# Seven half products in place of eight for queries, keys and gate of a linear attention, one pair of heads ahead

## The chip, the cores and the metric

The kernel runs on one core of a Trainium2 chip, as one launch. The metric is the device time of the whole program in microseconds (us). An engine name is short for: PE = TensorE matmul, PEld = its weight load, DVE = VectorE, ACT = ScalarE, POOL = GpSimd, SP = SyncE, which issues all the DMAs here. Each engine runs its own instructions in order and waits on semaphores for the others.

## What is computed

Six layers follow one another on x of 1024 tokens (8 blocks of 128) by 512, each with a layer norm ahead and a residual sum behind it. The change is in the fourth, the linear attention with 32 heads of 128:

```python
x = x + _L1_attn_ref(_layernorm(x, axis=-1), qkv_w, out_w, gate_w, norm_w)
# in it:
qkv = silu(h @ qkv_w.T)                     # queries, keys, values, 32 heads x 128
scores = q @ k.T * diag_decay               # the decay and the state together: one 128-wide block here
attn = scores @ v + (q * q_decay) @ kv
xf = attn * rsqrt(mean(attn * attn) + EPS)
gate = sigmoid(h @ gate_w.T)
return gate * (norm_w * xf) @ out_w.T
```

Behind it come a cross attention (`l1x`, which reads the context `ctx_4096` again) and a quantised projection (`l1f`). Ahead of it stand the layers `taylor`/`ffn`, `l0x` and `l0f`.

## The kernel before

**Numbers in two parts.** Every fp32 operand of a large product is split into a high part, rounded to the matmul type, and a low part, the rest. `mm3` then issues three matmuls, high by high, high by low and low by high (L556, L557, L558). For weights the high part `w_hi` is an ACT copy of the loaded tile `raw` (L1147), the low part `w_lo` a POOL subtraction (L414). Five slots of 128x1024 hold weights; SP loads slot s again once its `w_lo` is done.

**Stage `l1a`.** It runs over 16 pairs of heads (`HG = 16`), each in two halves of 512 tokens (`hf`). In a half PE does, in the order of the table `L1A_STEPS`: F0 to F3, the queries and keys of two heads (12 matmuls of 512 columns each), F4 and F5, the gate (12 each), S, the scores of four blocks, F6 to F9, the values of four blocks (12 matmuls of 256 columns each); and between them V0 to V3 and O0 to O3 of the half before: V is weights by values for one block (L892), O its share of the output (6 matmuls of 512). `halves` writes the loop: half 1 of pair i, then half 0 of pair i+1.

The two PSUM banks `pj` take all the F products in turn. For queries, keys and values ACT takes the sigmoid into `side` (`F`, L1308) and DVE multiplies it by the bank (L1915), which frees the bank; for the gate ACT's sigmoid (L1304) frees nothing and DVE multiplies by `norm_w` in SBUF (L1910). A block's V goes: DVE multiplies `pv` by the gate (L1929), ACT rounds it (`act_hi`, L1316) and squares `pv` (L1318), DVE makes `act_lo` (L1933) and adds the squares (L1935). O waits for `act_lo`, and DVE adds O's bank to `y` (L1446).

**What sets the order.** All is written out by hand: a program order for each engine, semaphores between them, one loop over the pairs on each engine. POOL's loop has five `w_lo` a pair and nothing else. At the stage's start PE goes on from `l0f` straight into F0, since the first 512 tokens are turned by then; at its end the V and O of the last half stand between the first products of `l1x` (`values_turned`, `keys`).

Of the kernel before, what the change touches and what calls it, by code (L numbers as in the profile page):

```python
# [42 lines left out]
PJ_PER = dict(ln=B, taylor=4, ffn=FG * 8, l0x=HG * 16, l0f=2 * B, l1a=HG * 20, l1xv=4, l1f=4)  # L43
# [16 lines left out]
L1A_STEPS = [("F", 0), ("V", 0), ("F", 1), ("O", 0), ("V", 1), ("F", 2), ("O", 1), ("V", 2), ("F", 3), ("O", 2),  # L60
             ("V", 3), ("F", 4), ("O", 3), ("F", 5), ("S", 0), ("F", 6), ("F", 7), ("F", 8), ("F", 9)]
# [48 lines left out]
L0X_SLOTS, L0F_SLOTS, L1A_SLOTS = (3, 4, 0, 1), (2, 3, 4, 0, 1), (3, 4, 0, 1, 2)  # L110


def build(nc, a):
    ctx = ExitStack()
    with ctx:
# [10 lines left out]
        WH = sb("w_hi", [P, NSLOT, PIECE], F32R)  # L126
        WL = sb("w_lo", [P, NSLOT, PIECE], F32R)
        X = sb("x", [P, B, D])
# [3 lines left out]
        with ExitStack() as shared:  # L132
            KW = shared.enter_context(nc.sbuf_tensor("keys_whole", [P, 2, T], FP32))
        CH = sb("ctx_hi", [P, KC, T], F32R)
        CL = sb("ctx_lo", [P, KC, T], F32R)
# [6 lines left out]
        with ExitStack() as shared:  # L142
            AF = shared.enter_context(nc.sbuf_tensor("act_whole", [P, 3072], FP32))
        AH = sb("act_hi", [P, NA], F32R)
# [4 lines left out]
        with ExitStack() as shared:  # L149
            TW = shared.enter_context(nc.sbuf_tensor("turned_whole", [P, NTW, 512], FP32))  # L150
        AL = sb("act_lo", [P, NA], F32R)
# [39 lines left out]
        with ExitStack() as shared:  # L191
# [55 lines left out]
            sem(n) for n in ("y_zero", "la_sg", "la_gt", "la_sqa", "la_gfhi", "la_gflo"))  # L247
        la_ss, la_v, la_a, la_y = sem("la_ss"), sem("la_v"), sem("la_a"), sem("la_y")
# [18 lines left out]
        def heads_of(which, h, j):  # L267
            return QK[:, 2 * which + h, j * S:(j + 1) * S]

# [37 lines left out]
        def nth(base, i, per, j):  # L307

            return i * per + (base + j), (base + j) % 2

# [15 lines left out]
        def _(sp):  # L326
# [77 lines left out]
        def _(pool):  # L404
# [92 lines left out]
            for s in (3, 0):  # L497
                split_lo(s, SLOT["l1x"][s])
# [53 lines left out]
        def _(pe):  # L552
# [296 lines left out]


            def l1a_half(now, before):
                for kind, n in L1A_STEPS:
                    l1a_step(now, before, kind, n)
                    if not before and kind == "F" and n in (1, 2):

                        turn_rows(3, (2 * n + 2, 2 * n + 3))

            def l1a_step(now, before, kind, n):
                if now if kind in "FS" else before:
# [5 lines left out]
                    if kind == "F" and n == 0 and not before:  # L865
                        pe.wait_ge(lt_done, LT[3] + HB)
# [1342 lines left out]
```

## Time and profile before

| what | us |
|---|---|
| median of 3 runs | 2439.05 (2437.66 to 2440.36) |
| the profiled execution, its own time | 2432.68 |
| its span in the trace | 2430.8 |
| PE busy | 2359.2, 97% |
| DVE, ACT, POOL busy | 1257.8, 904.3, 666.2 (52%, 37%, 27%) |
| stage `l1a` on PE | 1206.2 to 2208.4 |
| one pair of it | 62.80 |

The page's matmul durations overlap, since matmuls are pipelined: a 512-column matmul is listed with some 0.39 us and the next starts 0.23 us behind it. What PE spends is read from the starts. "Idle before" names who ended a wait; a "<-issue" in front of a weight load is a wait whose releaser the profile does not name.

### The profile page before, as it was taken

To read this page: it belongs to the slowest core of one execution; us is meant where nothing else is said; L and a number is where in the kernel's file an instruction comes from. 1 tells how busy PE (TensorE), PEld (TensorE's weight loads), DVE (VectorE), ACT (ScalarE), POOL (GpSimd) and SP (SyncE) were. 2 spreads that over 40 slices of the span, in tenths; PEclk is the share of its full clock that TensorE was granted. 3 is DMA by queue.
4 is the path that set the end of the run, shared out by engine and by line. 5 is a ranking of instruction groups with operands and counts; after the bars stand their busy time and mean duration, and the time that the engine had idled before them with its cause. 6 is when DMAs were issued, how large, how long until landed. Compare 5 with 4: busy or idle time off the path is not lost.

```text
span 2430.8 us, 38454 instructions
## 1 busy us (share of the span) xinstructions
PE 2359.2 (97%) x13227; PEld 2013.1 (83%) x13227; DVE 1257.8 (52%) x2924; ACT 904.3 (37%) x2234; POOL 666.2 (27%) x381
## 2 busy tenths in 40 slices
PE   6999899999999999998999999999999999999898
PEld 5788688888888888887888888888888888887556
DVE  6544644445444444546654444444444444447786
ACT  2111344444444444443233333333333333333784
POOL 3444422322222232221231111111111111112462
PEclk9999999999999999999999999999999999999999
DMA  3210212111111211110111111111111111110000
GB/s 119 78 43 26 96 53 78 60 52 54 66 52 52 78 60 52 52 69 30 43 55 46 45 40 35 34 37 44 45 45 45 45 45 45 45 54 1 1 1 35
DMA packets 36832, 118.97 MB, mean 49 GB/s; under 512 B 4905, under 2 KB 7337, under 8 KB 36785
## 3 DMA queue, kind: packets, MB, share of 16 engines
q1 hardware_dynamic: 36784, 118.35, 14.2%
q8 instruction: 28, 0.46, 0.1%
q14 instruction: 20, 0.16, 0.0%
HBM read 116.24 MB, written 2.10 MB: 49 GB/s over the span
## 4 chain that ended last, share of the span: by engine, by line
PE 90%; DVE 5%; POOL 2%; ACT 2%; issue 1%; DMA 0%; POOLq 0%; SPq 0%; ACTq 0%; DVEq 0%
PE pj L556 19%; PE pj L557 19%; PE pj L558 19%; PE ou L556 7%; PE ou L558 6%; PE ou L557 6%; PE pv L746 2%; PE sc L883 2%; PE pv L892 2%; PE sc L730 2%; PE tp L737 1%; POOL w_lo L422 1%; DVE neg_max L2018 1%; POOL w_hi L420 1%; ACT probs L1371 1%
## 5 line engine op out<-in xcount | busy, mean ns | idle before, releaser
L414 POOL TENSOR_TENSOR w_lo<-raw,w_hi 128x1024 fp32r<-128x1024 f32 x145 | 346.9, 2393 | 1437.4 <-ACT w_hi L1147 1398.0
L556 PE MATMUL pj<-xt_hi,w_hi 128*128 128x512 f32 x1232 | 500.3, 406 | 6.9 <-DVE w_lo L1598 2.5
L557 PE MATMUL pj<-xt_lo,w_hi 128*128 128x512 f32 x1232 | 483.5, 392 | 0.0
L558 PE MATMUL pj<-xt_hi,w_lo 128*128 128x512 f32 x1232 | 483.0, 392 | 0.0
L556 PE MATMUL ou<-w_hi,act_hi 128*128 128x512 f32 x684 | 276.8, 405 | 4.5 <-ACT raw L1363 2.0
L556 PEld LDWEIGHTS pj<-xt_hi,w_hi 128*128 128x128 f32 x1232 | 233.9, 190 | 51.1 <-DVE w_lo L1598 2.9
L558 PEld LDWEIGHTS pj<-xt_hi,w_lo 128*128 128x128 f32 x1232 | 232.8, 189 | 49.8
L557 PEld LDWEIGHTS pj<-xt_lo,w_hi 128*128 128x128 f32 x1232 | 233.9, 190 | 41.2
L558 PE MATMUL ou<-w_hi,act_lo 128*128 128x512 f32 x684 | 267.6, 391 | 0.0
L557 PE MATMUL ou<-w_lo,act_hi 128*128 128x512 f32 x684 | 266.8, 390 | 0.0
L1446 DVE TENSOR_TENSOR x<-x,ou 128x512 f32<-128x512 f32 x192 | 130.8, 684 | 247.5 <-PE ou L558 247.1
L1308 ACT ACTIVATE side<-pj 128x512 f32<-128x512 f32 (+1 forms) x256 | 125.7, 491 | 340.8 <-PE pj L558 340.8
L1915 DVE TENSOR_TENSOR queries_keys<-side,pj 128x512 f32<-128x512 f32 x128 | 88.1, 688 | 184.1 <-ACT side L1308 184.1
L556 PEld LDWEIGHTS ou<-w_hi,act_hi 128*128 128x128 f32 x684 | 128.8, 188 | 50.0 <-issue 22.0
L1223 ACT ACTIVATE queries_keys<-pj 128x512 f32<-128x512 f32 x128 | 76.5, 598 | 245.2 <-PE pj L558 245.2
L556 PE MATMUL pj<-w_hi,xt_hi 128*128 128x256 f32 (+1 forms) x544 | 160.7, 295 | 2.5 <-DVE x_sum L1524 1.6
L1147 ACT ACTIVATE w_hi<-raw 128x1024 fp32r<-128x1024 f32 x146 | 153.6, 1052 | 20.5 <-PE ou L558 18.7
L558 PE MATMUL pj<-w_hi,xt_lo 128*128 128x256 f32 (+1 forms) x544 | 157.4, 289 | 0.0
L557 PE MATMUL pj<-w_lo,xt_hi 128*128 128x256 f32 (+1 forms) x544 | 157.3, 289 | 0.0
L558 PEld LDWEIGHTS ou<-w_hi,act_lo 128*128 128x128 f32 x684 | 128.7, 188 | 27.6
L556 PE MATMUL pj<-w_hi,ctx_hi 128*128 128x256 f32 x512 | 147.8, 289 | 0.7 <-POOL w_lo L422 0.7
L557 PEld LDWEIGHTS ou<-w_lo,act_hi 128*128 128x128 f32 x684 | 129.1, 189 | 23.3
(246 smaller groups left out, 4505.3 us busy)
## 6 DMA issues: line engine op xcount, KB each, us to landing
raw<-in_l1a_w SPq DMA_DIRECT2D x80, 512.0 KB, 4.2
raw<-in_l0x_w SPq DMA_DIRECT2D x64, 512.0 KB, 4.2
side<-in_side SPq DMA_DIRECT2D x32, 512.0 KB, 3.9
raw<-in_ffn_w SPq DMA_DIRECT2D x15, 512.0 KB, 3.3
raw<-in_l0f_w SPq DMA_DIRECT2D x6, 512.0 KB, 3.7
raw<-in_l1x_w SPq DMA_DIRECT2D x6, 512.0 KB, 3.5
raw<-in_taylor_w SPq DMA_DIRECT2D x5, 512.0 KB, 6.7
x<-in_x SPq DMA_DIRECT2D x2, 1024.0 KB, 7.3
```

Of the source, the lines that this page charges most:

```text
L414: pool.tensor_tensor(WL[:, s, :], RAW[:, s, :], f32(WH[:, s, :]), ALU.subtract).then_inc(w_ready[s], 1)
L556: pe.matmul(out, wh, xh, start=first, stop=False)
L557: pe.matmul(out, wh, xl, start=False, stop=False)
L558: return pe.matmul(out, wl, xh, start=False, stop=last)
L730: last = pe.matmul(score(j)[:, h * S:(h + 1) * S], heads_of(0, h, j), heads_of(1, h, j), start=True, stop=True)
L746: last = pe.matmul(pv[:, h * S:(h + 1) * S], VT[:, n, h * S:(h + 1) * S], TA[:, n % 2, h * S:(h + 1) * S], start=True, stop=True)
L883: last = pe.matmul(score(j)[:, h * S:(h + 1) * S], heads_of(1, h, j), heads_of(0, h, j), start=True, stop=True)
L1147: act.activation(WH[:, s, :], RAW[:, s, :], ACT.Copy).then_inc(w_hi[s], 1)
L1223: act.activation(QK[:, n, :], bank[:], ACT.Copy, scale=S ** -0.5 if n < 2 else 1.0).then_inc(pj_done, 1)
L1308: act.activation(F[:, x % 2, 0:w], pj[bank][:, 0:w], ACT.Sigmoid).then_inc(la_sg, 1)
L1446: dve.tensor_tensor(dst, dst, ou[bank][:], ALU.add).then_inc(x_done, 1)
L1915: dve.tensor_tensor(dst, F[:, x % 2, 0:w], pj[bank][:, 0:w], ALU.mult).then_inc(pj_done, 1)
```

## The change

**Products.** For queries, keys and gate the 512x256 weights of a pair are cut into four blocks of 256x128, and the 1024 tokens into two halves: a 2x2 by 2x2 block product. It was eight half products of 6 matmuls each and is now seven (P1 to P7, Winograd's form): three take sums of weight blocks (P3, P5, P6), four take sums of token halves (P4 to P7). The values stay as they were.

- *Token sums*, once: DVE writes four sums of 128x(2x512) (`tokens_whole`), ACT rounds them (`tokens_hi`), DVE takes the rest (`tokens_lo`). They lie where the split context lay.
- *Weight sums*, each pair and each of the three slots: POOL makes the third sum (L625), ACT copies 768 and 256 columns (L1600, L1601, `opened`), POOL makes the low parts (L630, L631) and three further sums in place (L636, L638, L640), ACT rounds 768 columns of them (L1608), POOL takes their rest (L645). `sums_hi` and `sums_lo` are one buffer for all three slots.
- *Output sums*: a product lands in one of three banks (`pj0`, `pj1`, `tp`). ACT copies P1 to `seventh`, and DVE adds seven times for each kind: c11, sixth, with_seventh, c21, c22 (two), c12. Sigmoid and multiplication then take the finished blocks from SBUF.

**Order.** PE's loop has an odd part (queries and keys of pair i+1, and V, O, values R4 to R7 and scores of pair i) and an even part (the rest of the keys and the gate of pair i+1, its scores and values R0 to R3, and V and O of pair i's second half). So queries, keys and gate run one pair ahead.

**Space.** x is written to the output array and its place used for the new tiles; it is read back behind the scores of the last pair. The context is loaded and split again behind the last gate.

The core of the diff:

```diff
+L1A_FILLS = ["P1q", "P2q", "P6q", "P7q", "P4q", "P5q", "R4", "P3q", "P1k", "R5", "P2k", "P6k", "R6", "P7k", "P4k",
+             "R7", "P5k", "P3k", "P1g", "P2g", "P6g", "R0", "P7g", "R1", "P4g", "R2", "P5g", "R3", "P3g"]
...
+            sp.wait_ge(la_gs, 4 * HG)
+            for c in range(KC):
+                sp.dma_start(CR[:, c, :], a["ctx_t"][c]).then_inc(c2_in, 16)
...
+            def product(name, s, out, first):
+                n, moving = (SUMS_OF if name in SUMS_OF else BLOCKS)[name]
+                for kk in range(2):
...
+                    last = mm3(out[:], w, x, first and kk == 0, kk == 1)
...
+                V(0)
+                seventh(i, "P3k", 4, p)
+                seventh(i, "P1g", 1, p)
+                O(0)
+                V(1)
+                seventh(i, "P2g", 1, p)
+                seventh(i, "P6g", 1, p)
+                O(1)
...
+            def c22(i, kind):
+                dve.wait_ge(*full(i, "P5" + kind))
+                b = fill(i, "P5" + kind)[0]
+                dve.tensor_tensor(target(kind, "12"), value_bank[b][:], P7[:], ALU.add).then_inc(la_v5, 1)
+                dve.wait_ge(*taken(i, "P4" + kind))
+                dve.tensor_tensor(target(kind, "22"), value_bank[b][:], target(kind, "22"), ALU.add).then_inc(fb_done[b], 1)
...
             tail("V", 0)
             sums(0)
             ready(0, SLOT["l1x"][0])
+            pe.wait_ge(c2_ready, KC)
+            pe.wait_ge(fb_done[1], fill(HG - 1, "R5")[2])
+            pe.wait_ge(la_fm, event(HG - 1, "R7") + 1)
             values_turned(0)
```

**POOL, the loop over the pairs, before.** The five low parts of a pair:

```order
L414 TENSOR_TENSOR w_lo<-raw,w_hi 128x1024 x2
L413 REGISTER_ALU
L414 TENSOR_TENSOR w_lo<-raw,w_hi 128x1024 x2
L413 REGISTER_ALU
L414 TENSOR_TENSOR w_lo<-raw,w_hi 128x1024
```

The second half of that loop now, from the third sum of slot 3 (queries, next pair) over the low part of slot 2 (output weights) to slot 4 (keys, next pair). The loop then begins again with the `sums_lo` of slot 3:

```order
L625 TENSOR_TENSOR w_sums<-raw 128x256
L629 ISA
L630 TENSOR_TENSOR w_lo<-raw,w_hi 128x768
L631 TENSOR_TENSOR w_lo<-w_sums,w_hi 128x256
L635 ISA
L636 TENSOR_TENSOR raw<-raw 128x256
L637 REGISTER_ALU
L638 TENSOR_TENSOR raw<-raw 128x256
L639 REGISTER_ALU
L640 TENSOR_TENSOR raw<-raw 128x256
L550 REGISTER_ALU
L551 TENSOR_TENSOR w_lo<-raw,w_hi 128x1024
```

Five instructions of one width a pair became two of that width and 21 narrower ones.

**ACT, the last half before the stage's tail, before.** Values, a weight copy, and then the tail's first block at once:

```order
L1308 ACTIVATE side<-pj 128x256 x4
L1147 ACTIVATE w_hi<-raw 128x1024
L1316 ACTIVATE act_hi<-side 128x256
L1318 ACTIVATE side<-pv 128x256
```

The same place now:

```order
L1624 ACTIVATE side<-pj 128x256
L1624 ACTIVATE side<-tp 128x256
L1624 ACTIVATE side<-pj 128x256
L1464 ACTIVATE w_hi<-raw 128x1024 x2
L1745 ACTIVATE ctx_hi<-ctx_again 128x1024 x4
L1464 ACTIVATE w_hi<-raw 128x1024 x2
L1645 ACTIVATE act_hi<-side 128x256
L1647 ACTIVATE side<-pv 128x256
```

Two weight copies and four context copies moved in between the last values and the tail. On POOL two `w_lo` and four `ctx_lo` of 128x1024 answer to them, and PE's `values_turned` waits for the fourth.

## Rows read from the trace of the kernel before

**Rows 1.** The page's line of busy time, share of the span and instructions.
```profile
PE 2359.2 (97%) x13227; PEld 2013.1 (83%) x13227; DVE 1257.8 (52%) x2924; ACT 904.3 (37%) x2234; POOL 666.2 (27%) x381
```

**Rows 2.** The window of 14 pairs: us, busy us of PE, PEld, DVE, ACT, POOL; clock.
```profile
1262.50:2141.70 879.20, 879.20 (x4930) 763.64 (x4929) 414.87 (x840) 288.85 (x574) 167.34 (x70) 1.00 0.13 44
```

**Rows 3.** Timeline of SP: one decay load a pair (start, us, what).
```profile
1262.48 0.33 SPq L393 DMA_DIRECT2D decay<-in_decay  x1
...
2141.69 0.33 SPq L393 DMA_DIRECT2D decay<-in_decay  x1
```

**Rows 4.** Timeline of PE in pair 4: V, then F, O and values.
```profile
1500.00 0.60 PE L892 MATMUL pv<-probs,values 128*128 128x128 f32 x4
...
1500.67 0.40 PE L557 MATMUL pj<-xt_lo,w_hi 128*128 128x512 f32 x1
...
1502.95 0.39 PE L558 MATMUL pj<-xt_hi,w_lo 128*128 128x512 f32 x1
1503.27 0.49 PE L556 MATMUL ou<-w_hi,act_hi 128*128 128x512 f32 x1
...
1509.40 0.28 PE L557 MATMUL pj<-w_lo,xt_hi 128*128 128x256 f32 x1
1509.52 0.28 PE L558 MATMUL pj<-w_hi,xt_lo 128*128 128x256 f32 x1
```

**Rows 5.** The same V on ACT, DVE and POOL.
```profile
1501.33 0.42 ACT L1316 ACTIVATE act_hi<-side 128x256 fp32r<-128x256 f32 x1 [0.95 <-DVE side L1929]
...
1500.80 0.42 DVE L1929 TENSOR_TENSOR side<-pv,gate 128x256 f32<-128x256 f32 x1
1501.78 1.36 DVE L1933 TENSOR_TENSOR act_lo<-side,act_hi 128x256 fp32r<-128x256 f32 x1 [0.56 <-ACT act_hi L1316]
...
1500.46 2.40 POOL L414 TENSOR_TENSOR w_lo<-raw,w_hi 128x1024 fp32r<-128x1024 f32 x1 [6.91 <-ACT w_hi L1147]
```

**Rows 6.** Two lines of DVE, 1300 to 2100: ns min/median/max.
```profile
L1933 DVE TENSOR_TENSOR act_lo<-side,act_hi x104: 425/426/1361, 1300.2 to 2098.4; 128x256 fp32r<-128x256 f32 x104
L1915 DVE TENSOR_TENSOR queries_keys<-side,pj x103: 687/689/689, 1301.8 to 2096.1; 128x512 f32<-128x512 f32 x103
```

**Rows 7.** DVE's `norm_w` products of the first pair, and POOL then.
```profile
1222.47 4.14 DVE L1910 TENSOR_SCALAR gate<-gate,norm_w 128x512 f32<-128x512 f32 x2 [2.03 <-ACT gate L1304]
...
1221.80 2.39 POOL L422 TENSOR_TENSOR w_lo<-raw,w_hi 128x1024 fp32r<-128x1024 f32 x1
```

**Rows 8.** POOL and ACT by line: busy, mean ns, idle before.
```profile
L414 POOL TENSOR_TENSOR w_lo<-raw,w_hi 128x1024 fp32r<-128x1024 f32 x64 | 153.0, 2391 | 642.6 <-ACT w_hi L1147 642.6
L1147 ACT ACTIVATE w_hi<-raw 128x1024 fp32r<-128x1024 f32 x64 | 67.4, 1053 | 9.9 <-PE ou L558 9.9
L1308 ACT ACTIVATE side<-pj 128x256 f32<-128x256 f32 x100 | 38.4, 384 | 132.5 <-PE pj L558 132.5
```

**Rows 9.** Other widths on POOL: timeline at 2202.80, and a line of the whole trace.
```profile
2202.80 1.28 POOL L495 TENSOR_TENSOR sumsq<-sumsq 128x512 f32<-128x512 f32 x1
...
L430 POOL TENSOR_TENSOR ctx_lo<-side,ctx_hi 128x1024 fp32r<-128x1024 f32 x4 | 10.4, 2594 | 0.3
```

**Rows 10.** Start of the stage on PE and DVE.
```profile
1206.21 0.39 PE L556 MATMUL pj<-xt_hi,w_hi 128*128 128x512 f32 x1
...
1211.66 1.04 PE L590 MATMUL sc<-identity,probs 128*128 128x128 f32 x8
...
1208.94 1.00 DVE L1515 TENSOR_SCALAR probs<-x,bn_mean_var,rstd 128x512 f32<-128x512 f32 x2
```

**Rows 11.** End of the stage on PE.
```profile
2208.39 0.71 PE L892 MATMUL pv<-probs,values 128*128 128x128 f32 x4 [0.93 <-DVE values L1915]
...
2209.75 0.48 PE L556 MATMUL pj<-ctx_hi,w_hi 128*128 128x512 f32 x1
```

**Rows 12.** A wait of PE before `l0f`, and the 5 us window behind it.
```profile
1119.25 0.68 PE L746 MATMUL pv<-probs_turned,values 128*128 128x128 f32 x4 [3.80 <-issue]
...
1120.00:1125.00 5.00, 5.00 (x25) 4.33 (x24) 3.85 (x10) 2.34 (x6) 0.00 (x0) 0.66 0.02 3
```

More of the change, by code:

```diff
@@ new lines, in value_row, with scores_l1a @@
+            def value_row(i, n):
+                out = bank_of(i, f"R{n}")[:, 0:256]
+                for c in range(KC):
+                    last = mm3(out, rows(XT, n)(c), wcols(0, 0, 256, 256)(c), c == 0, c == KC - 1)
+                last.then_inc(full(i, f"R{n}")[0], 1)
+            def scores_l1a(i, hf, free):
+                pe.wait_ge(*free)
+                pe.wait_ge(sc_done, i * B + (SC["l1a"] + hf * HB + 2))
+                for j in range(HB):
+                    at = slice(j * S, (j + 1) * S)
+                    for h in range(2):
+                        last = pe.matmul(score(j)[:, h * S:(h + 1) * S], head_half(1, h, hf)[:, at], head_half(0, h, hf)[:, at],
+                                         start=True, stop=True)
+                    last.then_inc(sc_full, 1)
@@ new lines, in weighted @@
+            def weighted(i, hf, n, ev):
+                t = i * B + (hf * HB + n)
+                if n == 0:
+                    pe.wait_ge(la_fm, ev + 1)
+                pe.wait_ge(sc_done, t + (SC["l1a"] + 3))
+                pe.wait_ge(pv_done, t + (PV["l1a"] + 1))
+                v = part(PR, 4 + n) if hf else VT[:, n, :]
+                for h in range(2):
+                    last = pe.matmul(pv[:, h * S:(h + 1) * S], v[:, h * S:(h + 1) * S],
+                                     part(PR, n)[:, h * S:(h + 1) * S], start=True, stop=True)
+                last.then_inc(pv_full, 1)
@@ new lines, in output_l1a @@
+            def output_l1a(i, hf, n):
+                t = i * B + (hf * HB + n)
+                m, bank = nth(OU["l1a"], i, B, hf * HB + n)
+                if hf == 0 and n == 0:
+                    ready(2, i + SLOT["l1a"][2])
+                pe.wait_ge(la_gflo, t + 1)
+                ou_free(m)
+                for h in range(2):
+                    last = mm3(ou[bank][:], both(A, lambda t: tile_b(t)[:, h * S:(h + 1) * S]),
+                               wcols(2, 0, 512, 512)(h), h == 0, h == 1)
+                last.then_inc(ou_full, 1)
@@ new lines, in l1a_even @@
+            def l1a_even(p, i):
+                old = i is not None
+                V = lambda n: gated(i, 1, n) if old else None
+                R = lambda n: row_value(i, n) if old else None
+                more = not (isinstance(p, int) and p == HG - 1)
+                V(0)
+                summed(i, "C22k")
+                first_out(i, "P1g", p * 3 + 2)
+                sums_hi(1, p, full(i, "P3k"))
+                summed(i, "C12k")
+                V(1)
+                gate(i, "11")
+                V(2)
+                R(0)
+                V(3)
+                if more:
+                    opened(3, p + 1)
+                R(1)
+                if old:
+                    act.wait_ge(ou_full, i * B + (OU["l1a"] + B))
+                    weight_hi(2, p + SLOT["l1a"][2])
+                gate(i, "21")
+                R(2)
+                gate(i, "22")
+                if more:
+                    opened(4, p + 1)
+                R(3)
+                gate(i, "12")
@@ L1962, in _ @@
             for n in range(HB):
[L1963 removed]
+                gated(HG - 1, 1, n)
                 if n == 1:
```

801 lines of the change are left out of this document (623 added, 178 removed).

## The prediction, made before the changed kernel ran

> **What bounds the kernel now.** I read the page's busy line first: PE is busy for 97% of the span, no other engine for more than 52% [rows 1]. Then the windows: in the fourteen pairs from 1262.50 to 2141.70 PE is busy for all of 879.20 us at the full clock, DVE for 414.87, ACT for 288.85, POOL for 167.34 [rows 2]. The decay loads, one a pair, are 879.21 us apart over 14 pairs, 62.80 each [rows 3]. So in this stage PE's own work is the time, and POOL has the most room. The timeline gives PE's prices by starts: ten steps from 1500.67 to 1502.95 make 0.228 us for a 512-column matmul; 0.12 for one of 256 (1509.40 to 1509.52) [rows 4]. V took 0.36, and 0.08 more on the matmul behind it.
>
> **What is removed.** Each of three kinds drops from 8 half products to 7, so 3 x 6 = 18 matmuls a pair, 288 in all: 288 x 0.228 = **65.7 us off PE**. A pair becomes 62.8 - 4.1 = 58.7 us of PE. That is the whole gain; the rest is what stands against it. A half product is 6 x 0.228 = 1.37 us, four values rows 1.44 each, O 1.37.
>
> **What is added, by engine.** DVE gets 21 additions of 512 columns a pair at most 0.69 each, like L1915 [rows 6]: 14.5 us on the 29.6 it has now (414.87 / 14). 44 of 58.7 us: not the bound by its sum. ACT gets three copies of 512 and three of 768: about 5 us on 20.6. POOL: 2.39 us for 1024 columns [rows 8] and 1.28 for 512 [rows 9] give 0.17 + 2.17 per thousand columns, so 0.73 for 256 and 1.83 for 768. A pair has two of 1024, six of 768 and fifteen of 256: 4.8 + 11.0 + 11.0 = 26.8 us, against 12.0 now. That too is under 58.7. So the sums of work say that all of it hides; what it costs where that cover is gone is the following. What decides is the order, since each engine is a queue. I walk through the places where PE waits last.
>
> **A. POOL's chain to the next pair, 2.1 us each loop pair.** I count from the start of V3 in the even part. Its `act_hi` starts 1.33 behind V's start [rows 5], and with the square ACT is free at about 2.0. Then ACT opens slot 3: 768 and 256 columns, 1.2 us by 1.05 for 1024 [rows 8] in two pieces: 3.2. POOL: 1.83 + 0.73 + three times 0.81 (0.73 and 0.08 for the semaphore) = 5.1: 8.3. The low part of slot 2, 2.4: 10.7. The third sum of slot 4, 0.73: 11.5. ACT, which has stood waiting for just that in `opened(4)`, copies 1.2 us: 12.7. Only then comes the sigmoid of R3 behind it, 0.38 [rows 8], DVE's multiplication, 0.42, and the semaphores: 13.7. PE needs R3 for V0 of the next pair and gets there, after V3, four products, three values rows and O3, at 0.44 + 5.48 + 4.32 + 1.37 = 11.6. Stall: 2.1. Bounds 1.4 (DVE's path through c22 and the gate, which ends about then too) and 2.8 (POOL's instructions held up by DVE's).
>
> **B. V0 behind the gate, 1.2 us.** R3's multiplication, then late, has the gate's last work queued behind it on DVE: a `norm_w` product, c12, ACT's sigmoid, another `norm_w` product. Only then comes V0's. By about 0.4, 0.69, 0.6, 0.4 and the V chain, O0 could start 3.7 us behind V0, and with both `norm_w` products waiting for POOL 5.0 (two of them took 4.14 us together beside a POOL subtraction, [rows 7]); PE has only P1 and P2 between, 3.2 with V. Stall 0.5 to 1.8; I take 1.2, between them.
>
> **C. The even part's O1 and P6, 1.6 us.** The one buffer for the rests of the sums lets `sums_lo` of slot 1 start only after P3k, and behind ACT's copy of P1g and of the sums: POOL ends it 0.4 us after PE could start P6g. Then POOL goes straight on to slot 0, and DVE has C12k's multiplication and V1's `act_lo` to do. What that costs is in [rows 5]: `act_lo` usually takes 0.43, yet started at 1501.78 under a POOL subtraction that ran to 1502.86 it took 1.36, and ended 0.28 us behind it; L1915, with one input in PSUM, never did (687 to 689 ns) [rows 6]. PE's O waited for it: 1503.27 instead of 1503.18 [rows 4]. Now queries and keys are multiplied out of SBUF too, and POOL is at work for 46% of the pair and not 19%. Walked: `act_lo` ends about 1.8 us late for O1. Bounds 0.3 (no collision, only P6g) and 2.6 (POOL's next instruction wins again); I take 1.6, as not every pair will hit it.
>
> The Trainium skill, "SBUF — State Buffer", section "Who interferes with whom", says the same as a rule: a DVE instruction with two SBUF inputs and a GpSimd one that reads SBUF exclude each other for the whole instruction, whichever starts first. By it each of the 24 such DVE instructions a pair (8 multiplications, 8 `act_lo`, 8 sums of squares) can be held up and can hold up POOL, and it speaks against this change; without it B would be 0.5 and C 0.3. The collision of [rows 5] agrees with it.
>
> **D. Other waits** (a bank not free, `sums_lo` of slot 4 before P6k with 1 us to spare): 0 to 0.8, I take 0.2.
>
> A to D: 5.1 us in each of 15 loop pairs (bounds 2.2 and 8.0) = **76.5 us** (33 to 120).
>
> **E. The stage's start, 18 us.** Before, PE goes from `l0f` into F0 at 1206.21 without a wait [rows 10]. Now P6q needs token sums of all 1024 tokens. DVE has the first rows of the second half ready at 1209.94 [rows 10]. Behind that stand, in its order, four 512-wide sums, four times four sums of 256 (1.8 us a block), rows and rests as before, values: the last sum is done near 1223.4. ACT's four copies of 1024 end at 1227.5, its copy of the weight sums stands behind them (1228.4), POOL's rest waits for the last of DVE's `tokens_lo` (1229.2) and ends at 1231. PE until then has four values rows, the turns (1.04 for two, [rows 10]) and two products: 10.6 us of 25. Stall 14.4. Behind it, with no V and O to fill, POOL's queue holds up P6k by 1.7 and P6g by 2.1. 18.2; bounds 10 and 22.
>
> **F. The last pair's first half, 8 us.** It has no products to put between V and O: the V chain is 2.3 us from V to O at best [rows 5], and twice DVE multiplies a values row first that PE only makes after V. 4 to 10.
>
> **G. The context, 14 us.** PE now waits ahead of `values_turned` until the context is split again. ACT has its copies behind the sigmoid of R7, the last values: one weight copy, 1.05; then POOL: two low parts, 4.8, and four `ctx_lo` at 2.39 to 2.59 [rows 8, 9], 9.6 to 10.4. About 16 us from R7; PE has V0 and the sums of squares, about 1.4 us (2208.39 to 2209.75, [rows 11]). 14; bounds 10 and 16. The DMA itself is issued some 24 us earlier and hides behind the last half; so does x's way back, which only the scaled sums behind it need.
>
> **H. The clock, 3 us.** After PE waited 3.80 us its clock over the next 5 us was 0.66 of full, that is partly at 1.2 GHz and not 2.4 [rows 12]: 1.7 us lost. E and G hold a longer wait each: 3.4, bounds 0 and 5.
>
> **The sum.** -65.7 + 76.5 + 18.2 + 8 + 14 + 3.4 = +54, on the profiled execution's 2432.68: 2487. The median of the runs stands 6.4 above that execution, so **2493**. All low bounds: -65.7 + 33 + 10 + 4 + 10 + 0 = -9; all high: +107.
>
> **Rivals.**
>
> *The loop hides its work.* E to H still cost 43, so the kernel is faster if A to D stay under 23 / 15 = 1.5 us a pair. For it: every sum of work is well under 58.7 us, and the three banks and the pair ahead give slack. Against: A alone is 2.1, from means over 64 instructions [rows 8]. Time: 0 to 1.2 a pair, 2416 to 2434. Chance 0.14.
>
> *Only POOL's chain holds,* as collisions with DVE are rare: 2 us a pair, 10 us over before, 2449. With nearby values (1.5 to 3.5): 0.26, of which 0.06 lie within 0.2% of before.
>
> *The forecast,* 3.5 to 7 us a pair: 2470 to 2520. 0.43.
>
> *Collisions feed each other:* DVE and POOL hold each other up, and a late V0 shifts every chain behind it: 8 us a pair, 2537. 0.17. It decides if DVE is held up more than about once in two of its two-input instructions.
>
> **How the numbers follow.** 0.2% (5 us) is about what a measurement of this kernel can tell from no change. Faster 0.14, same 0.06, slower 0.80. The range leaves out about half of the first rival and the top of the last: 2430 to 2548.
>
> **What would show it.** In the profile after: the decay loads 63.8 us apart (58.7 if the loop hides all, 61 if only A holds). PE should wait before V0 (L1115) of each odd part for DVE's values row, before O0 and the even O1 for `act_lo`, before P6g for `sums_lo`. POOL's busy share of the stage near 45%. `act_lo` and the multiplication of queries and keys should have a mean well over 0.43 and 0.69. One wait of 8 us or more before the first P6q and one of about 14 for `ctx_lo`, each with a lower clock behind it. I am wrong if the loads stand less than 60.5 apart; if ACT's copies in `opened(4)` end before PE reaches R3's end, A falls; if the wait for `ctx_lo` is under 5 us, G does.

## The result, and the profile after

The changed kernel takes 2528.88 us (median of 4 runs, 2526.1 to 2529.55), the kernel before beside it 2438.36 (4 runs, 2436.33 to 2440.36): a ratio of 1.0369, 95% interval 1.0351 to 1.0387. That is 90.5 us slower. The forecast was slower, 2493, and 2528.9 lies inside its range of 2430 to 2548. Between the profiled executions (2432.68 and 2529.31) it is 96.6 us, where the sum had 54.

In short: a pair of heads saves 4.1 us of matmuls and gains 7.0 us of waits and what comes with them, so it is 2.9 us longer; the start and the end of the stage add the rest.

First the page's busy line, against [rows 1]: PE fell from 97% to 93%, POOL rose from 27% to 37%. Below it the window over the same fourteen pairs as [rows 2] (columns as there: us, busy us of PE, PEld, DVE, ACT, POOL, clock), and the decay load at its end, against [rows 3] (the one at its start is at 1293.12).

```profile
PE 2349.1 (93%) x12939; PEld 1982.7 (78%) x12939; DVE 1555.0 (62%) x3284; ACT 977.3 (39%) x2383; POOL 932.5 (37%) x676
```

```profile
1293.12:2213.08 919.96, 854.99 (x4676) 725.42 (x4675) 658.97 (x1135) 346.24 (x700) 390.07 (x322) 0.98 0.13 42
```

```profile
2213.08 0.34 SPq L499 DMA_DIRECT2D decay<-in_decay  x1
```

919.96 / 14 is 65.71 us a pair; it was 62.80, and 63.8 was forecast. In this window PE is not busy for 65 us; before, it always was. POOL is busy for 42% of it, where near 45% was forecast. One pair of it on PE, only the matmuls that waited (start, us, what, idle before and who ended it):

```profile
1510.75 0.49 PE L763 MATMUL tp<-tokens_hi,sums_hi 128*128 128x512 f32 x1 [0.24 <-POOL sums_lo L645]
...
1513.82 0.51 PE L763 MATMUL ou<-w_hi,act_hi 128*128 128x512 f32 x1 [1.42 <-DVE act_lo L2376]
...
1534.87 0.71 PE L1115 MATMUL pv<-probs,values 128*128 128x128 f32 x4 [2.71 <-DVE values L2350]
...
1539.68 0.49 PE L763 MATMUL ou<-w_hi,act_hi 128*128 128x512 f32 x1 [1.29 <-DVE act_lo L2376]
```

By starts (from one matmul's start to the next, less its 0.228) the holes are 0.40, 1.59, 2.87 and 1.45 us, 6.3 a pair. They stand where steps C (P6g and the even O1), A (V0) and B (O0) put them. The trace's list of waits says how often, for 1300 to 2200 (us in all, times, longest):

```profile
PE pv L1115 <- DVE values L2350: 37.8, 14, 2.7
PE ou L763 <- DVE act_lo L2376: 23.8, 17, 1.4
PE tp L763 <- POOL sums_lo L645: 3.3, 14, 0.2
```

Now who was late for V0. These are DVE, ACT and POOL ahead of 1534.87:

```profile
1528.81 2.21 DVE L2364 TENSOR_SCALAR gate<-gate,norm_w 128x512 f32<-128x512 f32 x1
1530.94 0.68 DVE L2338 TENSOR_TENSOR gate_second<-tp,seventh 128x512 f32<-128x512 f32 x1
1531.55 0.68 DVE L2340 TENSOR_TENSOR gate_second<-tp,gate_second 128x512 f32<-128x512 f32 x1
...
1532.25 0.63 ACT L1637 ACTIVATE gate_second<-gate_second 128x512 f32<-128x512 f32 x1 [3.82 <-DVE gate_second L2340]
1532.79 0.83 ACT L1600 ACTIVATE w_hi<-raw 128x768 fp32r<-128x768 f32 x1
1533.52 0.40 ACT L1601 ACTIVATE w_hi<-w_sums 128x256 fp32r<-128x256 f32 x1
1533.83 0.36 ACT L1624 ACTIVATE side<-pj 128x256 f32<-128x256 f32 x1
...
1528.33 2.40 POOL L551 TENSOR_TENSOR w_lo<-raw,w_hi 128x1024 fp32r<-128x1024 f32 x1
1530.69 0.93 POOL L625 TENSOR_TENSOR w_sums<-raw 128x256 f32<-128x256 f32 x1
```

The two copies of `opened(4)` (L1600, L1601) do stand ahead of R3's sigmoid (L1624). But ACT did not wait for POOL's third sum there: that was done at 1531.62. It had waited 3.82 us for DVE's c22 of the gate (ends 1532.23), the instruction ahead in its queue. And c22 was late since a `norm_w` product took 2.21 us, not 0.48 (its shortest time here), beside POOL's low part of slot 2.

The end of the stage, against [rows 11]. PE, POOL, and one of DVE's unpacking instructions there:

```profile
2298.11 1.87 PE L1238 MATMUL tp<-one,sumsq 128*128 128x1 f32 x8 [15.18 <-POOL sumsq L700]
...
2282.37 4.73 POOL L551 TENSOR_TENSOR w_lo<-raw,w_hi 128x1024 fp32r<-128x1024 f32 x2 [30.38 <-ACT w_hi L1464]
2287.07 9.59 POOL L694 TENSOR_TENSOR ctx_lo<-ctx_again,ctx_hi 128x1024 fp32r<-128x1024 f32 x4
2296.62 1.44 POOL L700 TENSOR_TENSOR sumsq<-sumsq 128x512 f32<-128x512 f32 x1
...
2282.44 2.60 DVE L1979 CAST w_bytes<-q_tmp 128x256 uint8<-128x256 int32 x1
```

PE stood 15.2 us, as step G had it, though one instruction earlier than it said: at the sums of squares, whose last part POOL does behind the four `ctx_lo`. POOL had been idle for 30.38 us before.

### The profile page after: what moved, and what is told of

It is laid out like the page before. It is cut to its first block, busy times and chain, and to the rows that moved or that the text cites. A ratio compares the mean times of both kernels' runs of the same rounds, so it can differ in the third digit from the quotient of the medians.

```text
span 2526.8 us, 39899 instructions
## 1 busy us (share of the span) xinstructions
PE 2349.1 (93%) x12939; PEld 1982.7 (78%) x12939; DVE 1555.0 (62%) x3284; ACT 977.3 (39%) x2383; POOL 932.5 (37%) x676
## 4 chain that ended last, share of the span: by engine, by line
PE 80%; DVE 10%; issue 3%; POOL 3%; ACT 3%; DMA 0%; DVEq 0%; ACTq 0%; POOLq 0%; SPq 0%
PE pj L763 14%; PE pj L764 14%; PE pj L765 14%; PE ou L763 7%; PE ou L765 6%; PE ou L764 6%; PE pv L953 2%; PE tp L763 2%; PE sc L1102 2%; PE sc L937 2%; PE pv L1115 2%; PE tp L765 2%; PE tp L764 2%; DVE act_lo L2376 1%; DVE keys_second L2350 1%
## 5 line engine op out<-in xcount | busy, mean ns | idle before, releaser
L551 POOL TENSOR_TENSOR w_lo<-raw,w_hi 128x1024 fp32r<-128x1024 f32 x100 | 245.5, 2456 | 686.9 <-ACT w_hi L1464 647.4
L763 PE MATMUL pj<-xt_hi,w_hi 128*128 128x512 f32 x622 | 263.6, 424 | 8.8 <-DVE w_lo L2027 2.5
L764 PE MATMUL pj<-xt_lo,w_hi 128*128 128x512 f32 x622 | 253.9, 408 | 0.0
L765 PE MATMUL pj<-xt_hi,w_lo 128*128 128x512 f32 x622 | 252.4, 406 | 0.0
L645 POOL TENSOR_TENSOR sums_lo<-raw,sums_hi 128x768 fp32r<-128x768 f32 x48 | 89.0, 1854 | 329.8 <-ACT sums_hi L1608 329.8
L630 POOL TENSOR_TENSOR w_lo<-raw,w_hi 128x768 fp32r<-128x768 f32 x48 | 88.0, 1833 | 264.0 <-ACT w_hi L1601 263.7
L763 PEld LDWEIGHTS pj<-xt_hi,w_hi 128*128 128x128 f32 x622 | 124.0, 199 | 35.1 <-DVE w_lo L2027 2.9
L765 PEld LDWEIGHTS pj<-xt_hi,w_lo 128*128 128x128 f32 x622 | 123.5, 198 | 27.7
L764 PE MATMUL pj<-w_lo,ctx_hi 128*128 128x256 f32 x512 | 144.9, 283 | 0.0
L765 PE MATMUL pj<-w_hi,ctx_lo 128*128 128x256 f32 x512 | 144.9, 283 | 0.0
L764 PEld LDWEIGHTS pj<-xt_lo,w_hi 128*128 128x128 f32 x622 | 124.1, 199 | 22.7
```

The costliest lines, as they stand in the source:

```text
L551: pool.tensor_tensor(WL[:, s, :], RAW[:, s, :], f32(WH[:, s, :]), ALU.subtract).then_inc(w_ready[s], 1)
L630: pool.tensor_tensor(WL[:, s, 0:768], RAW[:, s, 0:768], f32(WH[:, s, 0:768]), ALU.subtract).then_inc(ws_add[s], 1)
L645: pool.tensor_tensor(SL[:], RAW[:, s, 0:768], f32(SH[:]), ALU.subtract).then_inc(w_ready[s], 1)
L763: pe.matmul(out, wh, xh, start=first, stop=False)
L764: pe.matmul(out, wh, xl, start=False, stop=False)
L765: return pe.matmul(out, wl, xh, start=False, stop=last)
```

## The experiments

"A pair" below is the distance of the decay loads in the middle of the loop; it was 65.65 in the changed kernel.

**e1, POOL's `both_heads(0)` first.**

```diff
+            both_heads(0)
             split_lo(3, SLOT["l1x"][3])
...
-            both_heads(0)
```

> The changed kernel with one line moved: POOL adds the squares of the first half (both_heads(0), L700, 1.44 us) before the two w_lo and four ctx_lo, not behind them. In the changed kernel PE stood 15.18 us before sums(0), and the row names that POOL addition. Theory G (the re-split of the context is what is late, and PE's wait for ctx_lo stands right behind): PE passes sums(0) at once and waits before the first values_turned instead, for ctx_lo, some 14 us; the two waits together come down by 1 to 2 us at most (the addition and the eight small matmuls), the end of the stage comes 0 to 2 us earlier. Rival (the addition queued last is itself what PE waits for, the context is not): the wait is gone, 12 to 15 us less.

Measured: one run of 2520.3 us. PE's two waits in the tail, V0's and the context's:

```profile
2276.59 0.71 PE L1115 MATMUL pv<-probs 128*128 128x128 f32 x4 [1.36 <-DVE probs L2350]
...
2291.12 0.77 PE L763 MATMUL pj<-ctx_hi,w_hi 128*128 128x512 f32 x1 [13.03 <-issue]
```

The wait moved behind the sums of squares and kept 13.03 of its 15.18 us. The profile names no releaser for it; POOL's four `ctx_lo` end at 2291.02, 0.1 us ahead of that matmul. From the last decay load to the end of the span it is 312.4 us and not 313.7: 1.3 less. Theory G holds. (The rest of the difference to 2529.31 lies ahead of that load: 5.7 us ahead of the stage, and 1.2 in one pair of 66.8 us in the changed kernel, e6 below.)

**e2, the context's split in the last half.** On POOL the low part of slot 0 goes behind the context's; on ACT:

```diff
                     V(1)
+                    weight_hi(3, SLOT["l1x"][3])
                     V(2)
+                    ctx_hi(0, 1)
                     row_value(i, 4)
                     V(3)
+                    ctx_hi(2, 3)
```

> The changed kernel with the context's split moved forward: ACT copies slot 3's weights behind V1 of the last half and the four ctx_hi behind V2 and V3, POOL makes w_lo of slot 3 and the four ctx_lo there, where it was idle for 30 us, then both_heads(0) and w_lo of slot 0. Theory G: PE waits before the tail's sums and values_turned only for slot 0's copy and w_lo behind R7 (1.05 + 2.4 us, PE has 1.4 of its own), 2 to 3 us and not 15.4, and the low clock behind it is shorter: 12 to 17 us less than the changed kernel, about 2512 to 2517. If instead POOL's ctx_lo hold up act_lo in the last half by their own length (2.4 us each time), some of it comes back there: 6 to 10 us less. Rival (x read back or a weight load is what is late): nothing changes.

Measured: 2515.42 us, ratio to the kernel before 1.0326 (1.0309 to 1.0343), 13.5 below the changed kernel's median. From the last decay load to the end it is 303.9 us, 9.8 less; of the rest, 3.3 us lie ahead of the stage in the profiled executions, where nothing was changed. PE in the tail, and DVE's product of V0:

```profile
2281.22 0.80 PE L763 MATMUL pj<-ctx_hi,w_hi 128*128 128x512 f32 x1 [0.32 <-POOL w_lo L551]
...
2289.24 0.79 PE L763 MATMUL ou<-w_hi,act_hi 128*128 128x512 f32 x1 [3.48 <-DVE act_lo L2379]
...
2287.84 0.45 DVE L2375 TENSOR_TENSOR side<-pv,gate_second 128x256 f32<-128x256 f32 x1
```

The wait for the context is gone, 0.32 us are left. 3.5 us came back at once: DVE's unpacking stands ahead of V0's product, and the wait for the context had covered it. Also V0 itself waits 2.26 where it waited 1.36. So the wait of G was 15 us long, and taking it away gives 10: the forecast's 12 to 17 in the median, the 6 to 10 of its second case in the stretch itself.

**e3, R3's sigmoid ahead of `opened(4)`.**

```diff
                 gate(i, "22")
-                if more:
-                    opened(4, p + 1)
                 R(3)
                 gate(i, "12")
+                if more:
+                    opened(4, p + 1)
```

> The changed kernel with one move on ACT: at the end of the even part opened(4) (the two copies of the next keys' weights, 1.23 us) stands behind R3's sigmoid and the last gate sigmoid, not ahead of them. Theory of the prediction's step A (R3's sigmoid is late because ACT stands in opened(4), waiting for POOL's third sum): the wait before V0 of the odd part, 2.87 us a pair, shrinks by 2 or more, 15 pairs, 30 us less and more with the clock. Rival that the changed kernel's rows suggest (DVE's c22 of the gate, itself held up by a norm_w product of 2.21 us beside POOL, came after POOL's third sum: 1532.23 against 1531.62): only the 1.23 us of the copies leave the path; 1.0 to 1.3 us a pair off V0's wait, of which O0 may give back some, since the norm_w products still stand there: 8 to 20 us less in all.

Measured: 2529.89 us, ratio 1.0387 (1.0370 to 1.0404); nothing gained, a pair 65.8. PE in one pair's odd part:

```profile
1529.74 0.71 PE L1115 MATMUL pv<-probs,values 128*128 128x128 f32 x4 [1.69 <-DVE values L2350]
1534.53 0.49 PE L763 MATMUL ou<-w_hi,act_hi 128*128 128x512 f32 x1 [1.34 <-DVE act_lo L2376]
1539.38 0.49 PE L763 MATMUL tp<-tokens_hi,sums_hi 128*128 128x512 f32 x1 [0.97 <-POOL sums_lo L645]
```

V0 waits 1.0 us less, as the rival had it: only the copies left the path. The microsecond came back at P6q: opened later, slot 4 keeps POOL from `sums_lo` of slot 3. The prediction's wait for POOL's third sum was not what ended last, and the 30 us less that step A's theory expected did not come.

**e4, the `norm_w` products.**

```diff
                 R(2)
-                gate_weight(p, 1)
                 c22(i, "g")
                 R(3)
-                gate_weight(p, 2)
+                gate_weight(p, 1)
                 c12(i, "g", u + 2)
-                gate_weight(p, 3)
...
                 V(0)
+                gate_weight(i, 2)
+                gate_weight(i, 3)
```

> The changed kernel with three norm_w products moved on DVE: that of the first half's second head behind R3's multiplication (it was ahead of c22), those of the second half behind V0 of the odd part (they were ahead of it; only the even part needs them). Theory of step B (they stand between R3 and V0's product): the wait before O0 (1.45 us a pair) goes, and c22 comes 2 us earlier, so V0's wait falls too. If c22 was what V0 waited for, V0's wait falls to what POOL's third sum leaves (1531.62 and not 1532.23: 0.6 us less). Together 2.0 us a pair: 30 us less. If collisions with POOL only move on to the next DVE instructions in the row (act_lo of V0, c11), 10 us or less.

Measured: 2507.5 us, ratio 1.0291 (1.0273 to 1.0308); a pair 64.55, 1.1 less, where 2.0 was expected. The same place:

```profile
1525.92 0.71 PE L1115 MATMUL pv<-probs,values 128*128 128x128 f32 x4 [1.42 <-DVE values L2350]
1529.66 0.50 PE L763 MATMUL ou<-w_hi,act_hi 128*128 128x512 f32 x1 [0.21 <-DVE act_lo L2376]
1535.90 0.49 PE L763 MATMUL ou<-w_hi,act_hi 128*128 128x512 f32 x1 [0.96 <-DVE act_lo L2376]
...
1530.33 2.93 DVE L2364 TENSOR_SCALAR gate_second<-gate_second,norm_w 128x512 f32<-128x512 f32 x2
```

V0 waits 1.3 less, more than the 0.6 expected, O0 1.1 less. But the two products then ran beside POOL's slot 4 work, took 2.93 us and not 0.9, and O1 waits 0.96 where it never waited. c22 was now done at 1523.0 and POOL's third sum at 1523.8, so here the prediction's chain does decide: the two chains lie 0.6 to 0.8 us apart.

**e5, POOL narrow.**

```diff
+            N = 8
...
+                pool.tensor_tensor(SL[:, 0:N], RAW[:, s, 0:N], f32(SH[:, 0:N]), ALU.subtract).then_inc(w_ready[s], 1)
```

> The changed kernel with POOL's work in the loop mostly left out: of the instructions of a pair the third sums and their low parts (6 of 256 columns) stay, all others (two of 1024, six of 768, nine of 256) are made 8 columns wide, so the low parts and sums are not computed there. POOL's 26.8 us a pair fall to some 7; order, semaphores, ACT, DVE and PE are the same. If POOL's time and its collisions with DVE are what the loop pays for (theory): the waits before V0, O0, O1 and P6g (6.3 us a pair) go almost all, decay loads 59 to 60.5 us apart (58.7 is PE's own work), DVE's act_lo and multiplications back to 0.43 and 0.69. Rival (ACT's queue and DVE's own 44 us of work set half of it): 62 to 64 us apart.

The kernel leaves out most of the low parts and sums, so its output is not the layer's. Measured: one run of 2457.93 us; a pair 60.73, a little above the theory's 59 to 60.5 and below the rival's 62. The window of fourteen pairs, and two lines of DVE (1300 to 2100; busy, mean ns), in this kernel and then in the changed one:

```profile
1289.67:2140.78 851.11, 831.23 (x4681) 714.59 (x4680) 573.17 (x1135) 348.10 (x700) 112.31 (x322) 1.00 0.13 45
```

```profile
L2410 DVE TENSOR_TENSOR act_lo<-side,act_hi 128x256 fp32r<-128x256 f32 x105 | 44.7, 426 | 59.0 <-ACT act_hi L1679 59.0
L2398 DVE TENSOR_SCALAR gate<-gate,norm_w 128x512 f32<-128x512 f32 x26 | 12.5, 480 | 0.0
```

```profile
L2376 DVE TENSOR_TENSOR act_lo<-side,act_hi 128x256 fp32r<-128x256 f32 x97 | 57.7, 595 | 54.5 <-ACT act_hi L1645 54.5
L2364 DVE TENSOR_SCALAR gate<-gate,norm_w 128x512 f32<-128x512 f32 x24 | 32.2, 1342 | 0.0
```

DVE's busy time falls from 658.97 to 573.17, 6.1 us a pair: that is what POOL held it up by. Only 1.17 us before V0 and 0.26 before O0 stay: c22 and, behind it in ACT's queue, the gate's sigmoid and the two copies. The run takes away the length of POOL's work and its hold-ups at once; e4 and e6, which move single instructions, part them. By the Trainium skill, "SBUF — State Buffer", section "Who interferes with whom", not only DVE's two-input instructions but also `copy`, `cast` and `tensor_scalar` in their two-port modes share POOL's port; the `norm_w` rows (a `tensor_scalar`, 480 against 1342 ns) agree.

**e6, slot 0's low part earlier.**

```diff
                 sums_lo(4, i + 1)
+                split_lo(0, i + (SLOT["l1a"][0] + 1))
                 sums_lo(1, i + 1)
-                split_lo(0, i + (SLOT["l1a"][0] + 1))
```

> The changed kernel with one move on POOL: w_lo of slot 0 (2.8 us as it ran) stands ahead of sums_lo of slot 1, in the time in which POOL waited 14.3 us for ACT, and not behind it. Theory of step C (POOL goes straight on from sums_lo into that w_lo and holds up the multiplication of C12k and V1's act_lo: 1.83 and 1.63 us in place of 0.69 and 0.43): the even part's O1 waits 0.2 and not 1.42, P6g's 0.24 stays, loads 64.2 to 64.5 us apart. Rival (sums_lo alone is enough to make act_lo late, the multiplication's 1.83 is its doing): O1 still waits 1.0 or more, loads 65.3.

Measured: one run of 2512.9 us; O1 waits 0.23 and P6g 0.24. Step C's theory holds. Its pairs come in two lengths, ten near 64.46 us and four near 65.65, so the mean is 64.79, above the expected 64.2 to 64.5. Three of them, then three of the changed kernel (the third number from the end is PE's granted clock):

```profile
1484.84:1549.31 64.47, 60.00 (x335) 50.76 (x334) 45.41 (x82) 24.73 (x50) 27.77 (x23) 1.00 0.12 43
1549.31:1615.01 65.70, 62.51 (x335) 53.09 (x334) 45.50 (x82) 24.73 (x50) 27.77 (x23) 0.95 0.12 42
1615.01:1679.47 64.46, 59.98 (x335) 50.76 (x334) 45.41 (x82) 24.73 (x50) 27.77 (x23) 1.00 0.12 43
```

```profile
1490.13:1555.75 65.62, 59.95 (x335) 50.77 (x334) 47.01 (x82) 24.73 (x50) 27.88 (x23) 1.00 0.13 42
1555.75:1621.40 65.65, 61.30 (x335) 51.92 (x334) 47.10 (x82) 24.73 (x50) 27.84 (x23) 0.97 0.13 42
...
2015.22:2082.04 66.82, 62.47 (x335) 53.10 (x334) 47.09 (x82) 24.73 (x50) 27.85 (x23) 0.95 0.12 41
```

Behind the 2.7 us wait before V0 PE often runs at 1.2 GHz for a while. In the changed kernel that costs nothing in ten of fourteen pairs (65.65 against 65.62 in the rows): the matmuls lose some 1.5 us, and O0 behind them, which waits 1.45 for `act_lo` anyway, takes it up. Where the low clock begins with V0 itself they lose some 2.7, and 1.2 us are left over; that is the pair of 66.82, and it makes e6's four long pairs. Behind the shorter waits of e3, e4 and e9 (1.4 to 1.7 us) no pair shows a low clock.

**e7, all of it in the loop, and the context.** The moves of e2, e4 and e6, and for A (the call of `opened(4)` at the end of the even part goes, and POOL ends its loop with slot 4's third sum alone):

```diff
                 sums_hi(3, p)
                 summed(i, "C11q")
+                opened(4, p)
                 V(1)
...
                 sums_lo(3, i + 1)
-                next_weights(1, i + 1, i)
+                keys_and_gate(i + 1, i)
```

where `keys_and_gate` is slot 1's third sum, then low parts and other sums of slot 4, then those of slot 1.

> Several moves together, nothing left out: the norm_w products as in e4, the slot 0 low part as in e6, the context as in e2, and opened(4) with POOL's low parts and sums of slot 4 moved into the odd part, behind C11q's sigmoid and sums_lo of slot 3 (only the third sum stays where it was). Theory (the loop pays for order, each wait has one of these causes): no wait before V0 and O0, 0.2 before O1: loads 60.0 to 61.0 us apart, 65.65 before that, 70 to 80 us less in the loop and 10 at the end: 2435 to 2455. Rival (POOL's work beside DVE's costs the same wherever it stands: what leaves V0 comes back as act_lo of V1 and V2 or sums_lo held up): loads 62.5 to 64 apart, 2475 to 2500.

Measured: 2434.51 us over 10 runs, ratio 0.9999 (0.9989 to 1.0008), just under the theory's 2435 to 2455: what the change had lost is back. A pair is 60.47, inside the theory's 60 to 61.

**e8, the last half too.** Order on PE there, and the unpacking behind the tail's blocks:

```diff
+                    V(0)
+                    R(4)
+                    O(0)
...
+                for v in ((2, 3), (4, 5), (6,), (7,))[n]:
+                    unpack(v)
```

> As the one before, and in the last pair's first half PE makes R4, R5 and R6 between V and O of a block and not behind V2 and V3; DVE's unpacking of quantised weights stands behind the V chains of the tail and not ahead of its first; the sums of squares behind values_turned. Theory of step F (V's chain has nothing beside it there, 8.6 us in all) and of what the context's wait had covered (twelve unpack instructions ahead of V0's product): 3 to 5 us less from the rows, 3 to 6 less from the unpacking: 6 to 11 below the kernel before it. Rival (the chain of V is bound by DVE and ACT, rows between don't shorten it; the unpacking only moves to O1 to O3): 0 to 3 less.

Measured: 2429.04 us over 10 runs, ratio 0.9976 (0.9966 to 0.9986), 5.5 below e7 and just under the 6 expected. From the last decay load to the tail's V0 it went from 69.8 us to 65.0, though V0 still waited 5.25, for R7's product behind an unpacking that took 2.49 us beside `ctx_lo`.

**e9, slot 4 alone moved,** the diff of e7 alone.

> The changed kernel with slot 4's opening alone moved: ACT's opened(4) stands in the odd part behind C11q's sigmoid, POOL's low parts and sums of slot 4 behind sums_lo of slot 3 and the third sum of slot 1. Nothing else. Theory (in e3 the two copies left V0's path but POOL's work on slot 4 then held up sums_lo of slot 3 by 1 us and act_lo by 1.2 us): V0 waits 1.7 as in e3 (DVE's c22 behind the norm_w product of 2.21 beside POOL's slot 2 low part decides, not POOL's third sum), but P6q does not wait and O0 waits 0.5 or less: loads 63.0 to 63.6 us apart, 65.65 before. If V0 still waits 2.7, the copies were never what was late; if 0.5 or less, POOL's sums alone were, as the prediction had it: 62 apart.

Measured: one run of 2500.34 us, a pair 63.80, just above the expected 63.6. The waits, 1300 to 2100:

```profile
PE pv L1126 <- DVE values L2360: 20.2, 12, 1.7
PE ou L774 <- DVE act_lo L2386: 18.4, 13, 1.4
PE tp L774 <- DVE act_lo_whole L2350: 3.1, 12, 0.3
PE tp L774 <- POOL sums_lo L645: 3.1, 13, 0.2
```

V0 waits 1.7 as in e3, and now nothing comes back at P6q or O0 (0.29 by starts); there is a small new wait of 0.27 us. The 1.42 of the even O1 is step C's. Alone e9, e4 and e6 save 1.85, 1.1 and 1.2 a pair (e6 in its shorter pairs), 4.15; in e7 together 5.2. V0 has two chains of nearly one length, and the last 1.7 us go only when both are shortened.

**e10, the weight sums ahead of the token sums at the start.**

```diff
             rows_hi(3, (6, 7))
+            act.wait_ge(x_saved, 32)
+            act.wait_ge(ln_x, 4 * B)
+            sums_hi(3, 0)
             row_value(None, 3)
...
             sums_lo(3, 0)
+            pool.wait_ge(la_tlo, 4)
             first_weights(1)
```

> The changed kernel with one order changed at the stage's start: ACT rounds the weight sums of slot 3 ahead of R3's sigmoid and the four copies of the token sums, so POOL makes their low part while DVE is at the token sums; POOL then waits with slot 1 until DVE's tokens_lo are done. Theory: of the 5.95 us before P6q the part behind the first tokens_lo is this queue (copies 3.9, weight sums 0.8, POOL 2.6); with it gone P6q waits only for the first tokens_lo, 0.5 to 1.5 us; 4.5 to 5.5 us less, the waits before P6k and P6g stay 1.4 and 2.05. Rival (the token sums on DVE are what is late, and P7q or P4q wait next): 2 us less or under.

In the changed kernel the first P6q, P6k and P6g waited:

```profile
1234.27 0.77 PE L763 MATMUL pj<-tokens_hi,sums_hi 128*128 128x512 f32 x1 [5.95 <-POOL sums_lo L645]
1248.14 0.47 PE L763 MATMUL pj<-tokens_hi,sums_hi 128*128 128x512 f32 x1 [1.40 <-POOL sums_lo L645]
1259.99 0.47 PE L763 MATMUL tp<-tokens_hi,sums_hi 128*128 128x512 f32 x1 [2.05 <-POOL sums_lo L645]
```

With e10's order:

```profile
1224.64 0.47 PE L764 MATMUL pj<-tokens_hi,sums_hi 128*128 128x512 f32 x1 [2.27 <-DVE tokens_lo L2510]
1238.92 0.47 PE L764 MATMUL pj<-tokens_hi,sums_hi 128*128 128x512 f32 x1 [2.15 <-POOL sums_lo L645]
1250.77 0.47 PE L764 MATMUL tp<-tokens_hi,sums_hi 128*128 128x512 f32 x1 [2.05 <-POOL sums_lo L645]
```

From the first decay load to the second it is 74.1 us and not 80.5: 6.4 less, where 4.5 to 5.5 were expected. Part of that is the clock: over the same 300 matmuls PE is busy for 60.91 us at a clock of 0.95, and for 65.44 at 0.87 in the changed kernel. e3's execution is the nearer one to compare with, since its start is that of the changed kernel but for the place of `opened(4)`, and its clock there is 0.94: 79.2 us, PE busy for 61.41. Against it the stretch is 5.1 shorter, and PE's idle time fell from 17.80 to 13.16 us. So the queue of three engines ahead of P6q was the cause of most of that wait, and the theory's size holds. Its places do not: P6q still waits 2.27 us, for the tokens themselves, where 0.5 to 1.5 were expected; P6k waits 0.75 longer than before; P2q and P1k wait 0.57 and 0.45, which they had not. The one run took 2523.95 us.

**e11, all moves.** e8 and e10, and in the even part:

```diff
-                first_out(i, "P1g", p * 3 + 2)
                 sums_hi(1, p, full(i, "P3k"))
+                first_out(i, "P1g", p * 3 + 2)
...
-                queries_keys(i, "C12k")
                 V(1)
+                queries_keys(i, "C12k")
...
-            sp.wait_ge(la_gs, 4 * HG)
+            sp.wait_ge(la_v5, 3 * HG)
```

> All moves of e8, and: the start as in e10; in the even part ACT rounds slot 1's sums ahead of its copy of P1g, and DVE multiplies C12k behind V1's product and not ahead of it; the context's DMAs are issued behind the last c22 of the gate and not behind the last gate sigmoid, its copies one block earlier, and no unpacking stands ahead of R7. Theory: P6g and O1 of a loop pair lose their 0.24 and 0.22 us (loads 59.7 to 60.1 apart, 60.47 before that: 6 to 11 us), the start gives 5, the last half and its tail 2 to 4: 13 to 20 us below e8's 2429, that is 2409 to 2416. Rival (what is moved meets the next wait of 0.2 to 0.3 us in the same place, as e3 did): 5 to 8 us less, from the start alone.

Measured: 2412.86 us (4 runs), the kernel before beside it 2435.79, ratio 0.9907 (0.9890 to 0.9923): 0.9% under the kernel before. Its page and window, and `act_lo`:

```profile
PE 2319.5 (96%) x12939; PEld 1966.5 (82%) x12939; DVE 1491.4 (62%) x3284; ACT 977.7 (41%) x2383; POOL 926.1 (38%) x676
```

```profile
1283.02:2114.70 831.68, 828.97 (x4677) 713.72 (x4676) 603.91 (x1135) 346.45 (x700) 383.61 (x322) 1.00 0.13 46
```

```profile
L2407 DVE TENSOR_TENSOR act_lo<-side,act_hi 128x256 fp32r<-128x256 f32 x108 | 65.2, 604 | 61.2 <-ACT act_hi L1672 61.2
```

A pair is 59.41 us, 3.4 under the kernel before, and the list of PE's waits for 1300 to 2100 names none. POOL does the work of the changed kernel, 383.61 us against 390.07, and `act_lo` is held up as much as there, 604 ns against 595 in the mean. The forecast of 2409 to 2416 held it, but in part because two misses cancel. Between the profiled executions of e8 and e11 the loop gave 14.7 us (6 to 11 expected), the start 5.4 (5 expected), and from the last decay load to the end e11 takes 297.0 us and not 293.1, 3.9 more where 2 to 4 less were expected: a wait of 2.21 us for POOL's `w_lo` now stands ahead of the context's first products.

## Why the prediction was right, and what it sized too low

The direction, the range and the places were right; the sum was 42 us short in the profiled executions (54 against 96). The median hides 6 of them, 36 are left: the prediction added 6.4 us, since the median before stood that much above the profiled execution, and behind the change the two differ by 0.4. That part of the nearness is luck.

**The loop, 28 us short.** A pair came out at 65.7 and not 63.8. Waits: A 2.87 us for the 2.1 predicted, B 1.45 for 1.2, C 1.99 for 1.6, D nothing. To that come 0.10 to 0.12 us which the matmul behind each wait takes longer, four times a pair, a term that the sum did not have, and 0.2 to 0.3 us that PE's own work exceeds the predicted 58.7 by. Together that is 1.9 a pair, 15 times: from V0 of the first loop pair to V0 of the last, 985.0 us for the forecast's 957.

**A was right in its place and half wrong in its cause.** "ACT, which has stood waiting for just that in `opened(4)`" is the step that failed: POOL's third sum had come 0.6 us earlier, and DVE's c22, which the prediction had as the lower bound of 1.4, ended last, as a `norm_w` product ahead of it was held up to 2.21 us by POOL's slot 2. The copies themselves and their place ahead of the sigmoid were on the path (e3, 1.0 us), and behind c22 the third sum is the next to end (e4, e9). Of POOL holding up DVE the prediction spoke in B and C alone. Nor has the wait one cause: with POOL's work nearly gone 1.17 us of it stay (e5).

**B and C** held in place and cause, and came out 0.25 and 0.4 us larger: e4 takes O0's wait away, by DVE's order, and e6 that of O1, by POOL's order alone. That POOL, released late, goes straight on into what DVE or PE needs next was seen again in e3.

**E, 18.2 predicted.** From the stage's start to P6q it is 24.6 us (1209.65 to 1234.27), where the prediction had 25; but it put all the idle time into one wait of 14.4. There are 5.8 us of holes in the turns (the transposes of the token rows) and 6.1 ahead of P6q, and some 2.3 us by which matmuls at a low clock took longer. "One wait of 8 us or more" did not show: 5.95. Behind it P6k and P6g wait 1.55 and 2.20 for the predicted 1.7 and 2.1. That makes holes of 15.7 us in all. The queue named for P6q's wait was right (e10). **F, 8:** 8.6, and 1.5 more ahead of the tail's V0.

**G, 14:** 15.4 and then a low clock; from V0's start to the first `std` of `l1x` the difference grew by 18.7 us. e2 shows that the cause was right and that, with DVE's unpacking where it stands, a part would have been lost in any case.

**H, 3.4:** some 12 too low; this and the loop are the two terms that were mis-sized. The changed kernel's profiled execution reaches the stage 3.4 us later than the one before, and in `l1x` behind it loses 3.5 more, with a clock of 0.87 over 2373 to 2413. e1 reaches the stage at 1203.95 (the kernel before at 1206.21), and e6 takes 3.1 us less than the changed kernel behind that `std`, so these parts differ between executions and are no cost of a step. From the stage's start to the tail's V0, E and F came 5.4 over their terms where their waits are 0.4 under; G came 4.7 over, its wait 1.4. The 5.8 and 3.3 us left go with a low clock there (0.87 over 1212.60 to 1293.12, 0.85 over 2293 to 2333): by starts, matmuls below full clock took some 8 us longer in E and F and 2.4 behind the context's wait. That is more than is left, as some of it falls where PE would have waited anyway, and no run took the clock alone away.

**The rivals.** "The loop hides its work" failed by order and not by amount: with the same work in e11 it does. "Only POOL's chain holds" failed, as e4 and e6 show collisions to cost 1.1 and 1.2 a pair by themselves. "Collisions feed each other" came nearest in the time: 2528.9 lies above the forecast's own 2470 to 2520 and below this rival's 2537, though the pair, 7.0 us over the 58.7, is still at the forecast's upper end of 7 and not at 8. The sign that was to decide it did not show: `act_lo` took 595 ns in the mean but 426 in the median, and the multiplications of queries and keys 0.89 us in the mean and 0.69 for most, so fewer than one in two were held up. (By the prediction's own terms the time of "only POOL's chain" is 2447, not 2449.)

## What to carry to other kernels

When an engine in in-order queues gets many small jobs, sums of busy time say only what is possible: the same instructions took 65.7 or 59.4 us a pair by their order alone. Walk each chain to the instruction ahead in every queue it passes, and where two chains end within a microsecond, count on shortening both before the wait goes. Put work that holds up another engine (POOL's subtractions here) where that engine's late results have slack, and ask of every wait taken away what it had covered.

## What the runs showed of the hardware

- DVE instructions with SBUF input alone and only one input are held up by POOL's subtractions as well: the `norm_w` product 0.48 to 2.21 us, a cast of integers 0.47 to 2.60. Those with one of two inputs in PSUM (L2321) were not, 0.69.
- The total time lost to such collisions need not cost a loop anything: `act_lo` had a mean of 604 ns in the fastest kernel and 426 with POOL narrow, and in the fastest kernel PE is busy for 828.97 of the loop's 831.68 us.
- A spell at 1.2 GHz costs only what the next wait for another engine does not take up: nothing where the matmuls lost some 1.5 us ahead of a wait of 1.45 (65.65 and 65.62 us a pair), 1.2 us where they lost 2.7 (66.82).
